# The second attention of a gated block: float16 score halves turned by DMA instead of float32 tiles turned by TensorE

## The reference, cut to what matters

```python
x = x + tanh(g_xattn[1]) * attention(layernorm(x), ctx, ctx, wq, wk, wv)
# attention: 16 heads of 32, queries 2 x 2048, keys 2 x 154
scores = einsum('bhqd,bhkd->bhqk', Q, K) / sqrt(32)
attn = softmax(scores, axis=-1)
out = einsum('bhqk,bhkd->bhqd', attn, V)
```

## Time and profile before

| what | us |
|---|---|
| median of three runs | 2771.65 |
| the profiled execution, its own time | 2766.97 |
| its span | 2765.2 |
| first attention | about 0 to 440 |
| second attention: first scores | 1607.8 |
| second attention: last scores | 1923.4 |
| second attention: last row added to x | 1944.0 |

### The profile page before, as it was taken

How to read it: one execution, slowest core, us unless ns; L and a number is a source line. 1 busy time by engine, 2 the same in 40 slices (tenths; PEclk the granted TensorE clock), 3 DMA queues, 4 the chain that set the end, 5 groups by cost and what they waited for, 6 DMA issues and landing times. The chain is left out here.

```text
span 2765.2 us, 44090 instructions
## 1 busy us (share of the span) xinstructions
PE 2583.6 (93%) x16830; PEld 1404.4 (51%) x16830; DVE 1599.7 (58%) x2553; ACT 1390.0 (50%) x3074; POOL 1121.0 (41%) x887
## 2 busy tenths in 40 slices
PE   5788878999999999999999979998999999999999
PEld 3333333444444477777777645565444444444444
DVE  6799995655555365656556478887643332334232
ACT  4678884322322166666666468998433222222221
POOL 3577781565555656666666401011102211121111
PEclk8899999999999999999999989999999999999999
DMA  7799987222221299999999731322310111011000
GB/s 190 145 178 203 181 170 219 70 69 63 62 62 47 94 325 284 288 288 283 279 288 273 178 96 58 92 62 86 125 39 16 46 46 35 12 46 46 23 8 31
DMA packets 455409, 353.08 MB, mean 128 GB/s; under 512 B 323104, under 2 KB 332064, under 8 KB 455200
## 3 DMA queue, kind: packets, MB, share of 16 engines
q1 hardware_dynamic: 418336, 282.92, 36.6%
q0 software_dynamic: 36864, 67.34, 11.6%
HBM read 198.86 MB, written 75.89 MB: 99 GB/s over the span
## 5 line engine op out<-in xcount | busy, mean ns | idle before, releaser
L1673 POOL DMA_INDIRECT ids<-sh_tk,sh_su x256 | 267.8, 1046 | 231.0 <-PE sh_gu L55 75.0
L55 PE MATMUL ex_gu<-ex_xT,ex_h 128*128 128x256 f16 x3072 | 345.8, 273 | 2.3 <-ACT ex_xT L1946 1.7
L55 PEld LDWEIGHTS ex_gu<-ex_xT,ex_h 128*128 128x128 f16 x3072 | 300.1, 98 | 51.3 <-ACT ex_xT L1946 2.0
L2620 POOL TENSOR_TENSOR fe_prodT<-fe_pp,fe_prodT 128x512 f16<-128x512 f32 x64 | 77.4, 1210 | 591.3 <-ACT fe_prodT L2405 591.3
L2072 POOL DMA_INDIRECT xp<-ex_oo,ex_to x128 | 236.2, 1845 | 182.6 <-ACT ex_oo L1980 138.7
L1807 DVE SCALAR_TENSOR_TENSOR ex_h<-ring,ex_h 128x1024 f16<-128x1024 f32 x128 | 151.1, 1222 | 155.2 <-ACT ex_h L1797 155.2
L55 PE MATMUL at_g<-hm_zT,hm_w 128*128 128x512 f16 x768 | 184.7, 395 | 23.7 <-issue 16.1
L2536 DVE SCALAR_TENSOR_TENSOR ring<-fe_g,fe_nf,ring 128x512 f32<-128x512 f32 x32 | 24.0, 751 | 293.1 <-PE fe_g L2321 293.1
L55 PE MATMUL ex_o<-ex_h,ex_aT 128*128 128x512 f16 x768 | 181.2, 387 | 0.0
L1781 POOL DMA_INDIRECT ex_xg<-zrows,ex_idxu x128 | 158.3, 1237 | 49.2 <-issue 33.2
L650 ACT ACTIVATE at_s<-at_s,at_mx 128x154 f32<-128x154 f32 x512 | 168.5, 410 | 16.7 <-DVE at_mx L764 16.7
(11 more groups left out here) (361 smaller groups left out, 5560.4 us busy)
## 6 DMA issues: line engine op xcount, KB each, us to landing
ring<-L_ffn_expert_gate_up_w SPq DMA_DIRECT2D x64, 1024.0 KB, 8.0
ring<-L_ffn_expert_down_w SPq DMA_DIRECT2D x64, 512.0 KB, 9.1
ring<-x SPq DMA_DIRECT2D x24, 1024.0 KB, 6.5
x<-ring SPq DMA_DIRECT2D x16, 1024.0 KB, 5.0
zrows<-hm_zs SPq DMA_DIRECT2D x32, 256.0 KB, 2.3
xp<-ring SPq DMA_DIRECT2D x8, 1024.0 KB, 5.3
out<-ring SPq DMA_DIRECT2D x8, 1024.0 KB, 4.3
ring<-xp SPq DMA_DIRECT2D x7, 1024.0 KB, 5.7
```

The costliest lines, as they stand in the source:

```text
L55: mm = nc.tensor.matmul(out, lhs(a, k), rhs(b, k), start=start and i == 0 and j == 0, stop=stop and i == n - 1 and j == 2)
L1673: e.indirect_dma_start(ids, bass.IndirectOffsetOnAxis(slotu[b % 2][:, t, j:j + 1], 0), pair[b % 2][:, t, j, :], None, bounds_check=SLOTS - ...
L2620: e.tensor_tensor(prodT[:, 1, j, :], p32[q % 2][:, :], prodT[:, 0, j, :], ALU.subtract).then_inc(s["p_lo"], 1)
```

## The change

Exponentials are taken straight from PSUM for all eight heads; the copy at L1195 is gone. For it the scores have three half-unit pairs of banks (six banks) in rotation instead of two, and the general banks shrink from four to two. The exponentials go to a float32 buffer of three units (`at_s`); VectorE casts them to a high float16 half, GpSimd subtracts to get the low half, as in the first attention. In six of eight units both halves are turned by DMA; in units 3 and 7 of each eight (`by_tensor`) TensorE does it, as 20 float16 transposes in three banks' worth, copied out by VectorE, ScalarE and VectorE. V is kept as two float16 halves, and the product with V becomes three float16 terms. The layer norm's low half moves from VectorE to GpSimd. Each engine has a timetable of its own: every piece has a due time in units, and each engine's list is sorted by it.

```diff
-    NS = 2
-    NP = 3
...
+    NS = 3
+    NP = 2
...
-        gen = [ps(f"g{i}", [P, 512]) for i in range(4)]
-        Sh = [maps_ahead.gen[:, :, :].rearrange("p b (k n) -> p (b k) n", n=256), ps("S", [P, HG, 256])[:, :, :]]
+        gen = [ps(f"g{i}", [P, 512]) for i in range(2)]
+        Sh = [ps(f"S{i}", [P, HG, 256])[:, :, :] for i in range(2)]
+        Sh.append(maps_ahead.gen[:, :, :].rearrange("p b (k n) -> p (b k) n", n=256))
...
-        sc = [sb(f"s{i}", [P, HG, CTX], F32) for i in range(NS)]
-        prob = [sb(f"p{i}", [P, HH * (P + HD)], F32) for i in range(NP)]
-        pT = [sb(f"pT{i}", [P, HH + 2, BLK], F32) for i in range(2)]
+        sc = [sb(f"s{i}", [P, HH, CTX], F32) for i in range(NS)]
+        prob = [sb(f"p{i}", [P, 2, HH * (P + HD)], F16) for i in range(NP)]
+        pT = [sb(f"pT{i}", [P, 2, HH + 2, BLK], F16) for i in range(2)]
...
+            vector=dict(stats=(-13.23, -12.59), prepare=(-11.60, -11.32, -11.03, -10.30),
+                        finish=(13.41, 14.30, 15.61, 15.64)),
+            gpsimd=dict(low=(-11.20, -9.89, -9.38, -5.46), finish=(14.82, 15.51, 18.95, 20.13)),
...
+            def scores(i, part):
...
+                if 2 * i + part >= len(Sh):
+                    e.wait_ge(s["expd"], 2 * i + part - len(Sh) + 1)
...
+            def turn_keys(i, part):
+
+                out = bank(("t", i, part), left(i, part))[:, :].bitcast(F16)
+                if part == 0:
+                    e.wait_ge(s["p_hi"], i + 1)
+                else:
+                    e.wait_ge(s["p_lo"], i + 1)
+                for j in range(HH if part < 2 else 4):
+                    mm = e.transpose(out[:, j * P:(j + 1) * P], part_in(i, part, j), K.id16[:, :])
+                mm.then_inc(s["t_mm"], 1)
...
+            def high(i):
+
+                e.wait_ge(s["expd"], 2 * i + 2)
+                if i >= NP:
+                    e.wait_ge(*taken(i - NP))
+                if i < NP:
+                    e.wait_ge(s["blank"], NP)
+                e.tensor_copy(first_keys(prob[i % NP][:, 0, :]), sc[i % NS][:, :, 0:P])
+                e.tensor_copy(last_keys(prob[i % NP][:, 0, :]), rest_of(i)).then_inc(s["p_hi"], 1)
...
+            def rest(i):
+
+                rows = prob[i % NP]
+                e.wait_ge(s["p_hi"], i + 1)
+                e.tensor_tensor(first_keys(rows[:, 1, :]), sc[i % NS][:, :, 0:P], first_keys(rows[:, 0, :]), ALU.subtract)
+                e.tensor_tensor(last_keys(rows[:, 1, :]), rest_of(i), last_keys(rows[:, 0, :]), ALU.subtract
...
+            def turn_keys(i, low):
+
+                if not low and i % TPB == 0:
+                    reused(e, i)
+                e.wait_ge(s["p_lo" if low else "p_hi"], i + 1)
+                e.dma_start_transpose(pT[i // TPB % 2][:, low, :, i % TPB * P:(i % TPB + 1) * P], prob[i % NP][:, low, :]
+                                      ).then_inc(s[f"keys{i % NP}"], 16)
```

More of the change, by code:

```diff
@@ new lines, in second_attention, with pieces_of, first_keys @@
+        for engine, when in (("scalar", 1.5), ("vector", 1.5)):
+            for i in range(2):
+                at(engine, UNITS + when, "maps", 0, i)
+        for i, m in enumerate((-9.5, -4.5, 1.0, 5.3)):
+            at("sync", UNITS + m, "maps_ahead", 0, i)
+        def pieces_of(engine):
+            return [piece[1:] for piece in sorted(due[engine], key=lambda piece: piece[0])]
+        bank_of = {}
+        def first_keys(rows):
+            return rows[:, 0:HH * P].rearrange("p (h n) -> p h n", h=HH)
@@ new lines, in last_keys, with rest_of, taken @@
+        def last_keys(rows):
+            return rows[:, HH * P:].rearrange("p (j r n) -> p r j n", r=HG, n=HD)[:, :, :, 0:REM]
+        def rest_of(i):
+            return sc[i % NS][:, :, P:CTX].rearrange("p (r j) n -> p r j n", r=HG)
+        def taken(i):
+            if by_tensor(i):
+                return s["t_mm"], 3 * (i // EVERY + 1)
+            return s[f"keys{i % NP}"], 32 * sum(1 for j in range(i % NP, i + 1, NP) if not by_tensor(j))
+        def left(i, part):
+            name, before, each = (("t_vec", 0, 2), ("t_act", 0, 1), ("t_vec", 1, 2))[part]
+            return s[name], each * (i // EVERY) + before + 1
@@ new lines, in turn_keys, with values @@
+            def turn_keys(i, part):
[7 more added lines that the diff above has]
+                mm.then_inc(s["t_mm"], 1)
+            def values(B, u, gi):
+                n = 4 * B + 2 * u + gi
+                last = UPB * B + TPB * u + TPB - 1
+                g = B // NBB
+                e.wait_ge(s["v_out"], 2 * g + 2)
+                for parity in range(NP):
+                    e.wait_ge(*taken(max(i for i in range(last + 1) if i % NP == parity and not by_tensor(i))))
+                if by_tensor(last):
+                    for part in range(3):
+                        e.wait_ge(*left(last, part))
+                out = bank(("o", n), (s["o_hi"], n + 1))
+                ptb = pT[(2 * B + u) % 2]
+                grp = 2 * u + gi
+                heads = [(slice(j * HD, (j + 1) * HD), place(gi * HG + j)) for j in range(HG)]
+                for hv, hp in TERMS:
+                    for rows, k in heads:
+                        o = grp * P + rows.start
+                        e.matmul(out[rows, :], V[g][:, hv, o:o + HD], ptb[:, hp, k, :], start=(hv, hp) == TERMS[0], stop=False)
+                for hv, hp in TERMS:
+                    mm = e.matmul(out[:, :], VR[g][:, hv, grp, :], ptb[:, hp, HH + gi, :], start=False,
+                                  stop=(hv, hp) == TERMS[-1])
+                mm.then_inc(s["o_mm"], 1)
@@ L1131, in part_copy @@
[L1131 to L1148 removed]
+            for what in pieces_of("scalar"):
+                piece(*what)
```

377 lines of the change are left out of this document (171 added, 206 removed).

## The result

The changed kernel took 2786.92 us (median of 4 runs, 2785.4 to 2789.13), the kernel before 2769.38 beside it (2766.45 to 2780.64); the ratio is 1.0045 [1.0029, 1.0061]. I had said 2763, and the direction is the other one. The profiled execution took 2785.4 in its own time; its span of 2783.3 us is 18.1 longer than before.

The account below looks back on a forecast made before the run. No single engine bounded the kernel: TensorE, ScalarE and VectorE were nearly full. Blocks 1 to 5 -8.0, last steps -5.1, end +4.0, V split +0.7: sum -8.4, plus 4.7 to the median, 2763 us; own range 2752 to 2774, 8-in-10 2738 to 2792.

Parts of the forecast that it names:

- block 0: First block of the second attention: its entry is the same work, so 47.0 us, unchanged.
- The sums of the engines: Work per unit: TensorE 3.6, ScalarE 4.15, VectorE 3.7 before waits, GpSimd 3.74, DMA 4.0 us.
- The port: SBUF port shared by VectorE and GpSimd: casts and normalisations wait for GpSimd's running instruction, and GpSimd for them.
- the middle: Units 8 to 48, blocks 1 to 5: 4.8 us a unit instead of 5.0, -8.0 us.
- the pair's hold: Time per unit in which GpSimd or VectorE's casts and normalisations hold the shared port: 4.57 us.
- the rival at 2782: Port held in full without handover overlap, 4.95 us times 1.06, 5.2 a unit in the even part; chance 0.13.
- the loop's (2788): Return-loop rival: with two buffers, casts wait for earlier transposes to land; pace 5.3, 4.5 at the end; chance 0.15.
- With the factor 1.06, 4.8 us: Even part: a unit takes 1.06 times its fullest resource, the pair's 4.57 us, so 4.8 us.
- hidden there on average: VectorE's port waits under 0.9 us hide behind ScalarE's exponentials and small work; one of 2.0 does not.
- The end part: Last 15 steps, without low halves and normalisations: 4.15 to 4.2 us each against 4.54, -5.1 us.
- My mark for it: Sign of the return loop: VectorE's casts waiting for DMA landings over 30 us in all.
- The tail: After the last exponentials: an added cast, low half and wider copies, +4.0 us; last four additions stay 4.94.

Follow-up runs that it names:

- e1: Changed kernel plus three float16 filler products over unused score-bank columns ahead of each half's scores; 1.0039 of the kernel before.
- e3: Changed kernel without GpSimd's subtraction of 1024 columns (those low halves stay zero); 0.9958 of the kernel before.
- f1: Changed kernel with three buffers instead of two for the halves of the probabilities; 1.0026 of the kernel before.
- f2: Changed kernel with GpSimd's subtraction of 1024 columns split into two instructions of 512; 1.0055 of the kernel before.
- f3: Changed kernel with VectorE's row normalisations directly ahead of the unit's casts instead of ahead of its maxima; 1.0054 of the kernel before.
- g1: f1 with the third and fourth group of each block's query projection moved 0.8 and 0.95 units later on TensorE; 1.0032 of the kernel before.
- g2: g1 with the second turn of each TensorE unit also moved behind the next half's score products; 1.0036 of the kernel before.
- e2: Changed kernel with only 4 of the 12 products of each query projection in the second attention; 1.0008 of the kernel before.
- g3: f1 with TensorE turning one unit in eight instead of two, the DMAs turning the rest; 0.9983 of the kernel before.
- g4: f1, e2 and e3 in one: third buffer, shortened query projections, no subtraction of 1024 columns; 0.9857 of the kernel before.
- base_again: The changed kernel run once more, unaltered, as the measure of the first four follow-ups; 1.0046 of the kernel before.

## Why the prediction was wrong

**What bounded the kernel before** was read rightly; block 0 was not. I held its time to be the entry's and unchanged; it fell by 5.5 of 48.5 us, a gain that I had not counted. Why was not tested.

**The sums of the engines** were near enough. TensorE was forecast at 3.6 a unit and took 4.26 (170.57/40) at the fallen clock: "it stays below the others" was not true of its busy time. Holding the clock at 1.00 gained 3.5 us at most, net of the fillers (e1). ScalarE 4.13 (forecast 4.15), GpSimd 3.82 (3.74), VectorE 4.13 with its port waits (3.7 and up to 0.8). DMA 0.84 of 5.09, 4.3 (4.0).

**The port** was sized rightly, and it is what the middle is full of: the pair's hold was forecast at 4.57 us a unit, 3.74 of GpSimd and 0.83 of VectorE, and measured 4.62, 3.82 and 0.80. When the long subtraction goes, 14.4 us of VectorE's three lines go with it, 0.36 a unit, and the pace falls by 0.42 (e3). A longest of 2.44 stands where I said near 2, and a mean cast of 0.85 where I said 1.0 to 1.3. The rule of the Trainium skill's page "SBUF — State Buffer", section "SBUF: two separate sides", is that whoever starts first has the pair for its whole instruction while the other is blocked. The trace agrees that it is blocked, but there is some overlap at the handover (the normalisation above ended 0.29 us behind the subtraction and takes 0.54 undisturbed), and the hold is 4.62 and not the 4.95 of the rival at 2782. That this rival and the loop's (2788) come near the measured 2787 is luck of their sums: neither has the mechanism of the whole.

**The step that failed** is "With the factor 1.06, 4.8 us", put on the pair's 4.57. I took the factor from stretches with one to three engines at 89 to 94%, and had no row for what a pair of engines at one port leaves idle. It came out as 1.10: 5.09 for 4.62 in the middle, and 4.45 for 4.06 in the end part once the loop is out of the way (f1). Against 4.8 the middle is 11.5 us too long: about 2 are the pair's size, 2 the rounding of 4.84 to 4.8, and 7 the factor. So a unit is as long as before: the fullest resource, the pair, holds 4.62 us of it at a share of 91%, where TensorE had 4.71 at 94%.

For 0.46 us of a unit neither engine holds the port; the forecast left room for 0.23. In this time the queues, each in order, wait for one another. Moving pieces or cutting one wait did not reduce it in a way that the pace shows (f2, f3, g1, g2); taking work out of TensorE's queue did (e2, g3), and taking it off the port did more (e3, g4). In the same step I had the waits on VectorE "hidden there on average"; ScalarE's 20.9 us behind the maxima, 2.4 before, say they were not.

**The end part** is the larger miss: 4.2 forecast for it with the loop left out, 4.98 measured. f1 gives 0.53 of it to the return loop, 7.9 us in all; the other 0.25 is again the factor and the pair's size (3.9 forecast, 4.06 in f1). I had the loop as a rival, and by its time (2788) it came closest; but its place was wrong. I let it bind on the layer norms' transposes in the middle, where f1 shows that it cost nothing, and gave it a gain at the end, where it costs 7.9 us. My mark for it, over 30 us of casts waiting for landings, was a poor one: 27.6 us were measured (29.3 in base_again), and with 0.6 left in f1 the kernel gained only 0.2%.

**The tail**: +7.8 for +4.0. The subtraction and the waits that it brings are 4.2 (e3), the third buffer returns 1.4 (f1, 26.7); the last of the former:
```profile
1940.21 0.69 DVE L1225 CAST at_p<-at_s 128x1024 f16<-128x1024 f32 x1 [2.62 <-DMA at_pT<-at_p]
...
1956.34 4.95 POOL L1288 TENSOR_TENSOR ring<-ring,at_sv 128x512 f32<-128x512 f32 x4 [8.18 <-DVE at_sv L1259]
```
The last four additions are the 4.94 of the earlier trace rows. TensorE's clock may hold the rest:
```profile
1920.00:1960.00 40.00, 28.39 (x183) 15.99 (x182) 20.48 (x34) 17.08 (x64) 23.68 (x17) 0.60 0.70 182
```
It stood at 0.60 there (0.96 from 1920 to 1960 before), TensorE having stood idle for 3.28 and 2.62 us ahead of its last turned halves; what that costs was not separated. The entry's +3.2 for +0.7 wasn't either.

By terms the forecast of -8.4 missed by +2.5 (entry), -5.5 (block 0), +11 (middle), +14 (end part) and +4 (tail), and with +0.9 behind the last addition comes out at the 18.1 that were measured.

## What to carry to other kernels

When two engines hold one port in turn, add their times up as one resource before looking at any engine's share. Here no engine was above 84%, and the port was held for 91% of the time; the change had put a resource at 91% in the place of one at 94%, and a unit took as long. A factor on the fullest resource is a measurement of one kernel: an error of 0.04 in it (7 us) was nearly the whole gain forecast for the middle (8 us). Visible waits between in-order queues are not prices: moving pieces about did not change the time, leaving out or handing over work did, and so did one buffer more where a DMA closes the loop. And look for the loop where the pace is highest, not only where the most work is.

## What the runs showed of the hardware

- A copy of 1024 float16 from PSUM took 0.68 us on VectorE and 1.02 on ScalarE, one of 512 0.40 on VectorE (I took 1.7 for both of VectorE's together; 1.08 measured). A float16 transpose on TensorE cost 0.087 us (200 in 17.4) where the float32 one cost 0.163; the clock was 0.89 and 1.00 in the two stretches.
- GpSimd and VectorE's casts and normalisations from SBUF exclude each other but for a short handover: a normalisation that met the start of a subtraction took 2.44 us and ended 0.29 behind it, where 0.54 is usual. VectorE's maxima, read from PSUM, took 0.77 to 0.80 us throughout.
- Halving GpSimd's subtraction cost 0.2 us with what it waited: 2.27 for two of 512 columns (1.13 each), 2.06 for one of 1024.
- Less work on TensorE lowered its granted clock, from 1.00 to 0.89 in the middle, and to 0.82 in e2; filler products raised it to 1.00, with TensorE's busy share at 84% and 95%. In e2 the shorter queue gained in spite of the lower clock.
- With DMA at 0.98 in the middle (g3) the units ran faster than with 0.85 (f1), 4.89 for 5.04, and in the end part with 1.01 as fast as with 0.99 (4.46 and 4.45): a full DMA share alone does not set the pace when three buffers cover the landings.
